# First pass of a fused linear-attention and FP4 kernel: the pieces of four weight quantizations are laid into other tiles

## The reference

```python
xn = layernorm(x)                                  # no affine
# branch 1: linear attention with 16 heads of 64, then an FFN
Q, K = elu(xn @ Wq + bq) + 1, elu(xn @ Wk + bk) + 1
KV   = einsum('bshd,bshm->bhdm', K, xn @ Wv + bv)
Z    = 1 / (einsum('bshd,bhd->bsh', Q, K.sum(1)) + eps)
o    = einsum('bshd,bhdm,bsh->bshm', Q, KV, Z) @ Wo + bo
h    = layer_norm(xn + o, g1, be1)
s    = layer_norm(h + gelu(h @ W1 + b1) @ W2 + b2, g2, be2)
# branch 2: FFN whose activations and weights are rounded to FP4, blocks of 16
lin(a, w) = fp4(a) @ fp4(w).T
g    = silu(lin(silu(lin(xn, w_gate)) * lin(xn, w_up), w_down))
out  = x + s * g
```

## Time and profile before

| | |
|---|---|
| median of three runs | 1750.94 us (1749.17 to 1752.48) |
| the profiled execution: its time | 1750.24 us |
| its span, first to last instruction | 1748.4 us |
| PE, DVE, ACT, POOL busy | 96%, 76%, 55%, 40% of the span |
| chain that ended last | PE 61%, DVE 19%, issue 4%, ACT 3%, POOL 1% |
| mean granted TensorE clock | 0.992 |

### The profile page before, as it was taken

How to read it: one execution, slowest core, us unless ns; L and a number is a source line. 1 busy time by engine, 2 the same in 40 slices (tenths; PEclk the granted TensorE clock), 3 DMA queues, 4 the chain that set the end, 5 groups by cost and what they waited for, 6 DMA issues and landing times.

```text
span 1748.4 us, 30645 instructions
## 1 busy us (share of the span) xinstructions
PE 1674.7 (96%) x11203; PEld 1488.6 (85%) x11203; DVE 1321.7 (76%) x2698; ACT 968.9 (55%) x1757; POOL 697.6 (40%) x514
## 2 busy tenths in 40 slices
PE   6989999999899999999999999999999999999997
PEld 5768778888789898988998898988899898989896
DVE  6755755546668787979797887979797887879794
ACT  5555655656446555464646465554646464555643
POOL 3543443434133343434443433434333433344344
PEclk9999999999999999999999999999999999999999
DMA  6412312232400101020110102010100201010100
GB/s 202 145 61 68 120 53 97 80 124 73 139 1 1 49 1 49 1 100 6 45 49 1 49 1 100 1 49 2 49 26 25 91 10 49 1 49 1 49 1 24
DMA packets 65962, 89.33 MB, mean 51 GB/s; under 512 B 4235, under 2 KB 50455, under 8 KB 64790
## 3 DMA queue, kind: packets, MB, share of 16 engines
q1 hardware_dynamic: 65814, 87.38, 14.9%
HBM read 53.29 MB, written 34.08 MB: 50 GB/s over the span
## 4 chain that ended last, share of the span: by engine, by line
PE 61%; DVE 19%; issue 4%; ACT 3%; POOL 1%; DVEq 0%; POOLq 0%; ACTq 0%
PE QH L77 8%; PE QH L79 8%; PE QH L78 8%; PE AC L77 5%; PE AC L78 5%; PE AC L79 5%; PE GU L77 4%; PE GU L79 3%; PE GU L78 3%; DVE rl L1817 2%; DVE hb L1671 2%; DVE QH L1808 2%; DVE hb L1673 2%; ACT rh L1134 2%; PE DN L77 2%
## 5 line engine op out<-in xcount | busy, mean ns | idle before, releaser
L2285 POOL TENSOR_TENSOR hb<-hb,rs_h 128x704 f32<-128x704 f32 x64 | 89.0, 1391 | 327.2 <-DVE rs_h L1680 327.2
L1134 ACT ACTIVATE rh<-QH 128x512 fp32r<-128x512 f32 x256 | 150.5, 596 | 105.1 <-DVE QH L1808 103.5
L1823 DVE TENSOR_TENSOR rl<-QH,rh 128x512 fp32r<-128x512 f32 x128 | 85.2, 675 | 129.7 <-ACT rh L1134 103.0
L77 PE MATMUL GU<-wgh,xqh 128*128 128x352 f32 x448 | 148.4, 331 | 6.5 <-DVE hb L1673 4.9
L2290 POOL TENSOR_TENSOR hb<-hb,sn_h 128x704 f32<-128x704 f32 x64 | 89.1, 1392 | 163.9 <-DVE hb L1685 163.9
L78 PE MATMUL GU<-wgl,xqh 128*128 128x352 f32 x448 | 145.4, 324 | 0.0
L79 PE MATMUL GU<-wgh,xql 128*128 128x352 f32 x448 | 145.2, 324 | 0.0
L77 PE MATMUL AC<-Mh,rh 128*128 128x256 f32 x512 | 145.1, 283 | 0.0
L77 PE MATMUL AC<-w2h,rh 128*128 128x256 f32 x512 | 144.5, 282 | 0.0
L1147 ACT ACTIVATE QH<-QH,cols 128x512 f32<-128x512 f32 x128 | 84.6, 661 | 105.8 <-PE QH L79 104.4
L78 PE MATMUL AC<-w2l,rh 128*128 128x256 f32 x512 | 143.1, 280 | 0.0
(11 more groups left out here) (220 smaller groups left out, 5626.0 us busy)
## 6 DMA issues: line engine op xcount, KB each, us to landing
xa<-in_L_attn_src SPq DMA_DIRECT2D x16, 512.0 KB, 4.0
xt_scratch<-xth SPq DMA_DIRECT2D x32, 256.0 KB, 2.5
xt_scratch<-xtl SPq DMA_DIRECT2D x32, 256.0 KB, 3.0
xb<-in_L_attn_src SPq DMA_DIRECT2D x16, 512.0 KB, 3.9
xnTh<-xt_scratch SPq DMA_DIRECT2D x32, 256.0 KB, 4.6
xnTl<-xt_scratch SPq DMA_DIRECT2D x32, 256.0 KB, 5.7
out<-x SPq DMA_DIRECT2D x16, 512.0 KB, 7.0
m_scratch<-mh SPq DMA_DIRECT2D x16, 256.0 KB, 2.4
```

What stands on the lines that cost most here:

```text
L77: e.matmul(outp, lh, rh, start=start, stop=False, skip_group_check=check)
L1134: e.activation(RH[j % 4][:], src, ACT.Copy).then_inc(S[sem], 1)
L1823: e.tensor_tensor(RL[j % 4][:], QH[:, (j % 2) * 512:(j % 2 + 1) * 512], f(RH[j % 4][:]), ALU.subtract).then_inc(S["gel"], 1)
L2285: e.tensor_tensor(hb, hb, spread(rs_h[i % 2][:], 44), ALU.mult).then_inc(S["hin"], 1)
```

## The change

The tables `turn_at`, `quant_at` and `split_at` get other tile numbers, `c_at` and `t_at` become six tables of their own, and `quant_round` is cut into `quant_up` and `quant_down`, so that its two operations can stand in different tiles. The second half of DVE's `split_w` gets its own table `rest_at`. No operation is added or taken away, and no size changes. ACT's `split_w` still reads `split_at`, so that it moves as well.

```diff
-        turn_at = {14: 0, 15: 1, 16: 2, 17: 3, 30: 4, 31: 5, 33: 6, ...
-        quant_at = {10: 0, 11: 1, 26: 2, 27: 3}
-        c_at = {t + 2: k for t, k in quant_at.items()}
-        t_at = {t + 2: k for t, k in quant_at.items()}
+        turn_at = {14: 0, 15: 1, 16: 2, 17: 3, 29: 4, 30: 5, 33: 6, ...
+        quant_at = {10: 0, 11: 1, 22: 2, 27: 3}
+        c_at = {12: 0, 14: 1, 24: 2, 30: 3}
+        up_at = {12: 0, 14: 1, 24: 2, 30: 3}
+        down_at = {12: 0, 15: 1, 24: 2, 31: 3}
+        in_at = {10: 0, 11: 1, 22: 2, 27: 3}
+        out_at = {12: 0, 15: 1, 24: 2, 31: 3}
+        rest_at = {3: 1, 6: 2, 8: 3}
...
-        split_at = {3: 1, 5: 2, 7: 3}
+        split_at = {3: 1, 5: 2, 8: 3}
```

More of the change, by code:

```diff
@@ L244, in spread @@
             return v.unsqueeze(2).broadcast_to([128, nb, 16])
-        turn_at = {14: 0, 15: 1, 16: 2, 17: 3, 30: 4, 31: 5, 33: 6, 43: 7, 45: 8, 46: 9, 47: 10, 49: 11}
-        quant_at = {10: 0, 11: 1, 26: 2, 27: 3}
-        c_at = {t + 2: k for t, k in quant_at.items()}
-        t_at = {t + 2: k for t, k in quant_at.items()}
+        turn_at = {14: 0, 15: 1, 16: 2, 17: 3, 29: 4, 30: 5, 33: 6, 43: 7, 45: 8, 46: 9, 47: 10, 49: 11}
+        quant_at = {10: 0, 11: 1, 22: 2, 27: 3}
[5 more added lines that the diff above has]
+        rest_at = {3: 1, 6: 2, 8: 3}
         kv_at, m_at = {3: 0, 5: 1}, {6: 0, 7: 1, 9: 2, 10: 3}
         load_at = {0: 1, 4: 2, 6: 3}
-        split_at = {3: 1, 5: 2, 7: 3}
+        split_at = {3: 1, 5: 2, 8: 3}
         W_LATER = {1: (Wq, wqh, wql, 2), 2: (W1, w1h, w1l, 2), 3: (W2, w2h, w2l, 8)}
@@ L1600, in quant_scale, with quant_up @@
                 e.reciprocal(rs, am).then_inc(S["A_qv"], 1)
-            def quant_round(k):
+            def quant_up(k):
                 a, c, _ = quant_w(k)
@@ L1605, in quant_round, with quant_down @@
                 e.scalar_tensor_tensor(a, c, GRID_LO, a, ALU.max, ALU.add).then_inc(S["A_qr"], 1)
+            def quant_down(k):
+                a, c, _ = quant_w(k)
                 w.wait_ge(S["A_qr"], 2 * k + 1)
@@ L1890, in late_dve @@
                     wq_less(i - 1)
-                if i in t_at:
-                    quant_round(t_at[i])
+                if i in up_at:
+                    quant_up(up_at[i])
+                if i in down_at:
+                    quant_down(down_at[i])
                 if i in quant_at:
@@ L1895, in late_dve @@
                 if i in split_at:
-                    n = split_at[i]
-                    m = W_LATER[n][3] // 2
-                    split_w(n, 0, m, 2 * m)
-                    split_w(n, m, 2 * m, 2 * m)
+                    m = W_LATER[split_at[i]][3] // 2
+                    split_w(split_at[i], 0, m, 2 * m)
+                if i in rest_at:
+                    m = W_LATER[rest_at[i]][3] // 2
+                    split_w(rest_at[i], m, 2 * m, 2 * m)
             ln_pair(0, 0)
@@ L2359, in extra_pool @@
                     wv_less(i - 6)
-                if i in t_at:
-                    quant_out(t_at[i])
-                if i in quant_at:
-                    quant_in(quant_at[i])
+                if i in out_at:
+                    quant_out(out_at[i])
+                if i in in_at:
+                    quant_in(in_at[i])
             rstd_of(0)
```

## The result

| | before | changed |
|---|---|---|
| median of the executions of the comparison | 1751.53 us (1749.17 to 1752.48, 4) | 1740.79 us (1740.09 to 1742.54, 4) |
| ratio, 95% interval | | 0.9942 (0.9925 to 0.9959) |
| profiled execution, its span | 1750.24, 1748.4 | 1740.13, 1738.3 |
| mean granted TensorE clock | 0.992 | 0.995 |
| PE, DVE, ACT, POOL busy | 96, 76, 55, 40% | 96, 76, 56, 40% |

The change makes the kernel faster by 0.58% (10.2 us by the ratio). The forecast was 1744.0 (1740.9 to 1748.3), so the direction and most of the mechanism came out as said. The size was 3 us short, and the median of 1740.79 lies 0.1 us under the lower end of the range; on the second occasion it was 1743.51, half a microsecond from the forecast. The median of all nine executions of the changed kernel is 1742.09.

The account below looks back on a forecast made before the run. PE bounds the kernel, so only its stops and slow-clock stretches count. The tile-by-tile terms sum to -6.8 (-6.9 unrounded), giving 1743.3 us from the profiled execution and 1744.0 as median, range 1740.9 to 1748.3.

Parts of the forecast that it names:

- tiles 7 to 9, stops: PE's stop before 65.94 goes, but both `w2l` halves in tile 8 spend the gain again: +0.1 us.
- tile 10, stop: Late `w_gate` and `w_up` loads delay `quant_scale(0)`, and PE's stop before the turn near 88 us becomes about 2.2: +0.7 us.
- tile 10, clock: PE's stop of about 2.2 us brings its clock down, like the earlier one of 2.06: +1.7 us, or 0.
- tile 12, stop: `quant_abs(1)` no longer stands ahead of `ex(13, 0)`, so PE's stop shrinks from 2.06 to about 1.5: -0.5 us.
- tile 12, clock: With the stop shortened to about 1.5 us, PE's clock should hold: -1.7 us, or 0.
- tile 14: Rounding 1 and `quant_out(1)` leave the place ahead of `rstd`, for which PE had waited 0.68: -0.7 us.
- tiles 28 to 30, stops: PE's stop of 3.44 goes with quantization out of tiles 28 and 29, and that of 2.26 behind late `rstd`: -5.6 us.
- tile 29, clock: The fallen clock behind PE's stop of 3.44 us goes with that stop: -1.7 us.
- Rival 2: New wait replaces those removed: `w2l` meets POOL in tile 8, or tile 30's stretched rounding stops PE; 1747 to 1749, chance 0.2.
- rival 4: Late `w_gate` and `w_up` loads stop DVE and PE, slower than before: 1751 us or more; chance 0.03.
- Rival 1: Tile 10's stop doesn't fall into the slow clock, or loads land early enough: 1741.5 to 1742.3 us; chance 0.18.
- Rival 3: The clock falls in both tiles 10 and 12: -5.2 us, 1745.7 us; chance 0.12.

Follow-up runs that it names:

- the second occasion: The changed kernel timed once more with no edit, against the kernel before: 1743.51 us, ratio 0.9951 (0.9939 to 0.9963).

## Why the prediction was nearly right

The terms are those of the prediction, with what the profiles show. "Stops" compares the profiled executions of before and after.

| step | forecast | shown |
|---|---|---|
| tiles 7 to 9, stops | +0.1 | 0.95 + 1.27 to 1.01 + 1.14: -0.1 |
| tile 10, stop | +0.7 | 1.54 to 2.29: +0.75 |
| tile 10, clock | +1.7 | +1.7, in 5 of 6 executions |
| tile 12, stop | -0.5 | 2.06 to 1.27: -0.8 |
| tile 12, clock | -1.7 | -1.7 (but 2.06 fell in 2 of 3 executions) |
| tile 14 | -0.7 | -0.7 |
| tiles 22, 26 | +0.2 | 0.30 to 0.30: 0 |
| tile 24 | +0.7 | +0.5 |
| tiles 28 to 30, stops | -5.6 | 3.44 and 2.26 gone: -5.7 |
| tile 29, clock | -1.7 | -1.7 |
| clock at 50 to 56 and 126 to 130 | not counted | -3.4 |
| start of the kernel | not counted | +1.5 |

The forecast column sums to -6.8, the column of what was shown to -9.7. The small stop of 0.36 that went too (below) and the rounding make the rest of the -10.1 between the two executions.

**The mechanism** is right at each place. `w2l` took 2.35 us (forecast 2.47) and did not meet POOL; the last load started at 81.9 (82.4) and DVE's first `am_w` at 84.45 (84.6); the turn came at 88.03 (88.3); the stop there was 2.29 (2.2). Rival 2 (a new wait in tile 8 or 30) is refuted by the empty stretch from 200 to 339 us, rival 4 by the landing of at most 2.5 us. Rivals 1 and 3 differ from the forecast only in the clock. Rival 1 is no rival of the change but of the execution: the stop of 2.28 to 2.29 fell in five profiled executions and not in the sixth. Rival 3 (both tiles fall) was in none: the stop of tile 12, up to 1.84 us, never fell in 11.

**The step that was too small** is the one that made a list of clock terms: "I therefore price a fallen clock at 1.7 us", from three stops, of which two had fallen. The price held (1.70 to 1.72 us behind 15 of the 16 stops that fell in the profiled executions, 3.4 behind one), but not the list. Two stretches of the kernel before were missing from it, because I looked at the clock only behind the stops that the change touched; and whether a stop falls is no property of its length alone. The trace of the kernel before could have warned of this. Its stop of 2.44 before 125.00 had fallen, so 2.06 was not the only one near 2 us that did; its stop of 2.26 before 229.35, nearer to the forecast 2.2 than 2.06 is, had not (the window 229 to 235 us was granted 1.00). The choice of 2.06 as the model for tile 10 came true in five of six executions, which is luck as much as reading. The forecast was the sum for one set of falls, and the changed execution had another, 3.4 us better. That the median of four came out so low is therefore partly chance. The sum of stops was forecast at -5.1 and came to -6.0 for the same places (a small one of 0.36 before 249.30 went too; with rounding that makes the -6.3). These 1.2 us are what the forecast missed in every execution of the changed kernel; the rest of the miss goes with the execution.

**One step was right by its sum and wrong in its parts.** Tile 12's clock (-1.7) and tile 14's stop (-0.7) were taken as separate. They are one: without the half-clock stretch the stop of tile 14 is 2.28 to 2.29 (three kernels), with it 0.68. While PE works at half clock, what it is going to wait for goes on at its own pace. The two together are worth 2.3 to 2.4 us either way. The same holds at tile 7: the half clock at 50 to 56 us in the kernel before had shortened the stop of 0.95, which is 2.3 without it, so these terms, too, are not separate (numbers in the last section).

**What the W part is worth.** The prediction's terms for W1 and W2 alone were +0.1, +0.7 and +1.7, less a little in tile 12. The kernel with them alone measured +1.4, and the change without them -10.3 against -10.2 and -8.6 with them. This part of the change gains nothing by itself, and what it costs is under what these comparisons can tell.

## What to carry to other kernels

When steps of a side task are interleaved with a loop, first look for the handoff on which the loop's next round depends (here POOL's power for the norm, and ACT's exp behind an `abs` that waits) and keep it free of everything that takes a whole buffer: moving POOL's last step of two chunks from ahead of the power brought 3.7 of the 8.6 to 10.2 us. A stop that the profile gives to one releaser may have a second that ends two tenths of a microsecond earlier; read all inputs of the waiting instruction before paying for a move. And compare two kernels by the lengths of their stops, execution by execution, before comparing clocks: what the half clock takes changes from one execution of the same kernel to the next.
